# The same operations of a fused retention and FP4 feed-forward kernel in another order on all four engines

## What is computed

```python
q, k = rope(x @ Wq), rope(x @ Wk)
scores = einsum('bhqd,bhkd,hqk->bhqk', q * DQK ** (-0.5), k, decay)   # causal
o = einsum('bhqk,bhkd->bhqd', scores, v)
o = o * rsqrt(mean(o * o) + EPS) * g_norm_w
x = layernorm(x + (o * silu(x @ Wg)) @ Wo)
def fp4_quant_dequant(x):          # blocks of 16
    scale = max(abs(xb)) / 6.0
    return GRID[searchsorted(MID, abs(xb / scale))] * sign(xb) * scale
gate, up = fp4_linear(x, w_gate), fp4_linear(x, w_up)        # 128 -> 352
x = layernorm(x + fp4_linear(silu(gate) * up, w_down))       # 352 -> 128
```

## Time and profile before

| | |
|---|---|
| median of 3 runs | 142.82 us (141.59 to 142.87) |
| profiled execution | 142.74 us, of it the span 140.8 us |
| mean granted TensorE clock, share of full speed | 0.971 |
| PE busy | 125.6 us (89%) |
| DVE busy | 117.9 us (84%) |
| ACT busy | 99.6 us (71%) |
| POOL busy | 101.4 us (72%) |

### The profile page before, as it was taken

One profiled execution on the slowest core, in us unless ns is written; L12 is line 12 of the kernel. 1 busy time (PEld: TensorE's weight loads), 2 busy tenths in 40 slices (PEclk: granted clock), 3 DMA queues, 4 the chain that ended last, 5 costly groups with the idle time before them and its releaser, 6 DMA issues.

```text
span 140.8 us, 3621 instructions
## 1 busy us (share of the span) xinstructions
PE 125.6 (89%) x1232; PEld 81.4 (58%) x1232; DVE 117.9 (84%) x391; ACT 99.6 (71%) x311; POOL 101.4 (72%) x139
## 2 busy tenths in 40 slices
PE   4997898999999989999999899999997789985770
PEld 4864354755565655465566566565767577663650
DVE  1239987598588999999999999999999999999510
ACT  3054966768977778775977778787488689777643
POOL 4204198695997995887989598798967938874741
PEclk9999999999999999999999999999999999999855
DMA  4898970000000000000000000000000000002121
GB/s 122 243 240 244 416 232 3 0 9 0 5 0 0 7 0 0 7 0 0 5 0 2 0 5 0 0 7 0 5 0 0 19 19 2 19 0 79 37 74 56
DMA packets 6897, 6.53 MB, mean 46 GB/s; under 512 B 864, under 2 KB 6112, under 8 KB 6752
## 3 DMA queue, kind: packets, MB, share of 16 engines
q1 hardware_dynamic: 5856, 5.56, 13.3%
q10 hardware_dynamic: 1024, 0.76, 1.7%
HBM read 5.26 MB, written 1.05 MB: 45 GB/s over the span
## 4 chain that ended last, share of the span: by engine, by line
DVE 60%; PE 27%; issue 6%; ACT 2%; POOL 2%; POOLq 0%; DVEq 0%
DVE h_ratio L676 6%; DVE h_ratio L671 6%; PE ps L327 5%; DVE hs L663 5%; DVE h_blocks L821 4%; DVE h_ratio L680 4%; DVE probs L760 3%; PE ps L315 3%; DVE x_ratio L671 3%; PE ps L321 3%; DVE gate_o L780 3%; PE ps L377 2%; DVE x_ratio L676 2%; PE ps L344 2%; DVE ms L775 2%
## 5 line engine op out<-in xcount | busy, mean ns | idle before, releaser
L917 POOL TENSOR_TENSOR rstd_h<-ms,minus_half 128x8 f32<-128x8 f32 x16 | 27.1, 1695 | 9.2 <-DVE ms L775 9.1
L451 PE MATMUL ps<-wd_T,hT 128*128 128x128 f32 x96 | 15.5, 302 | 3.5 <-DVE r L803 2.8
L327 PE MATMUL ps<-w_vg,xT_sb 128*128 128x512 f32 x32 | 17.2, 619 | 0.6 <-DVE h_blocks L821 0.4
L908 POOL TENSOR_TENSOR qk<-rope_c,rope_s 128x256 f32<-128x256 f32 x16 | 12.3, 772 | 7.0 <-DVE rope_s L754 3.5
L944 POOL TENSOR_TENSOR hq<-h_ratio,hs 128x352 f32<-128x352 f32 x16 | 14.2, 898 | 3.6 <-DVE h_ratio L680 3.6
L451 PEld LDWEIGHTS ps<-wd_T,hT 128*128 128x128 f32 x96 | 13.3, 207 | 5.8 <-DVE r L803 3.1
L912 POOL TENSOR_SCALAR_AFFINE_SELECT probs<-raw 128x512 f32<-128x512 f32 x16 | 11.3, 705 | 5.7 <-ACT raw L493 5.7
L928 POOL TENSOR_TENSOR rstd<-veps,minus_half 128x1 f32<-128x1 f32 x16 | 9.6, 597 | 5.3 <-DVE veps L792 5.0
L437 PE MATMUL ps<-wgu_T,xqT 128*128 128x352 f32 x32 | 12.9, 484 | 0.6 <-DVE h_blocks L821 0.3
L431 PE MATMUL ps<-wgu_T,xqT 128*128 128x352 f32 x32 | 12.4, 470 | 0.1
L344 PE MATMUL ps<-q_eo,kT 32*128 32x256 f32 x128 | 11.4, 425 | 1.0 <-DVE gate_o L780 0.5
(11 more groups left out here) (112 smaller groups left out, 357.5 us busy)
## 6 DMA issues: line engine op xcount, KB each, us to landing
tabs_sb<-rope_tables SPq DMA_DIRECT2D x1, 1024.0 KB, 11.4
out<-x SPq DMA_DIRECT2D x16, 64.0 KB, 1.5
tabs_sb<-rope_tables SPq DMA_DIRECT2D x1, 640.0 KB, 7.9
xT_sb<-x_transposed SPq DMA_DIRECT2D x1, 512.0 KB, 9.2
x_res<-x SPq DMA_DIRECT2D x1, 512.0 KB, 11.9
xT_sb<-x_transposed SPq DMA_DIRECT2D x1, 320.0 KB, 6.9
...
```

What stands on the lines that cost most here:

```text
L327: mm(vg_ps, xT(c), w_vg[:], start=True, stop=True).then_inc(vg_pe, 1)
L451: last = mm(down_ps, hT[:, c % D, t, :], wd_T[:, t, :], start=t == 0, stop=t == 2)
L908: gp.tensor_tensor(qk[:, c % D, :], rope_c[:, c % D, :], rope_s[:, c % D, :], ALU.add).then_inc(qk_p, 1)
L917: gp.tensor_tensor(rstd_h[:, c, :], ms[:, c, :], minus_half[:], ALU.pow).then_inc(rms_p, 1)
```

## The change

Every engine's list is a permutation of the old one: no call is added, dropped or given other operands. In VectorE's and GpSimd's lists GpSimd's products and its select stand in other places relative to VectorE's steps with two operands in SBUF. Of the PSUM banks `yT` and `down` are exchanged (0 and 1), the gate weights' transposes move from bank 0 to 3, the up weights' from 3 to 0 and the down weights' from 2 to 3. In the diff "..." marks calls or lines left out.

```diff
-        BANKS = {"scV": (0, 1), "scA": (2, 3), "oT": (4, 5), "o": (2,), "yT": (0,), "qk": (7,),
+        BANKS = {"scV": (0, 1), "scA": (2, 3), "oT": (4, 5), "o": (2,), "yT": (1,), "qk": (7,),
...
-                 "up": (6,), "down": (1,), "U": (4,)}
+                 "up": (6,), "down": (0,), "U": (4,)}
...
-        wg_T_ps, wu_T_ps = ps[:, 0, 0:I], ps[:, 3, 0:I]
-        wd_T_ps = ps[:, 2, 0:384]
+        wg_T_ps, wu_T_ps = ps[:, 3, 0:I], ps[:, 0, 0:I]
+        wd_T_ps = ps[:, 3, 0:384]
...
-                occupy("wgu", (0, 3))
+                occupy("wgu", (3, 0))
...
-                occupy("wdt", (2,))
+                occupy("wdt", (3,))
...
# TensorE: the start and the end
-            project_vg(1); project_qk(1); scores(0); project_vg(2); project_qk(2); from_state(0); values(0)
-            transpose_qk(1); transpose_o(0); state_product(1); project_vg(3); scores(1); from_state(1)
+            project_vg(1); project_qk(1); scores(0); from_state(0); project_qk(2); project_vg(2); values(0)
+            transpose_qk(1); transpose_o(0); state_product(1); project_vg(3); transpose_qk(2); scores(1)
...
-            gate(14); up(14); down(10); transpose_xq(15); transpose_h(11); gate(15); up(15); transpose_h(12); down(11)
-            transpose_h(13); down(12); transpose_h(14); down(13); down(14); transpose_h(15); down(15)
+            down(8); gate(13); up(13); transpose_xq(14); down(9); gate(14); transpose_h(10); up(14); transpose_xq(15)
+            down(10); transpose_h(11); gate(15); up(15); down(11); transpose_h(12); transpose_h(13); down(12)
+            down(13); transpose_h(14); down(14); transpose_h(15); down(15)
...
# ScalarE: the start
-            silu_g_(2); copy_v(2); copy_oT(0); q_even(1); squares(0); weights_magic(1); q_odd(1); k_transposed(1)
+            copy_v(2); silu_g_(2); copy_oT(0); k_transposed(1); q_odd(1); weights_magic(1); squares(0); q_even(1)
...
# VectorE: the start
-            rope_sin_even(0); rope_cos(0); rope_sin_odd(0); next_state(0); weights_amax(0); rope_sin_even(1)
-            rope_sin_odd(1); rope_cos(1); weights_amax(1); mask_scores(0); weights_inv(1); rope_sin_odd(2)
-            rope_cos(2); rope_sin_even(2); weights_inv(0); weights_ratio(1); weights_ratio(0); gated(0)
-            weights_plus(1); next_state(1); weights_grid(1); mean_square(0); weights_value(1); mask_scores(1)
+            rope_cos(0); rope_sin_odd(0); rope_sin_even(0); weights_amax(0); weights_inv(0); next_state(0)
+            rope_cos(1); rope_sin_even(1); rope_sin_odd(1); weights_amax(1); mask_scores(0); rope_sin_odd(2)
+            rope_cos(2); rope_sin_even(2); weights_inv(1); weights_ratio(1); weights_ratio(0); weights_plus(1)
+            gated(0); mean_square(0); next_state(1); weights_grid(1); weights_plus(0); weights_value(1)
...
# VectorE: the end
-            h_product(13); ln2_sum(9); h_plus_(12); h_amax(13); h_grid_(12); h_inv(13); h_product(14); h_ratio_(13)
-            h_amax(14); ln2_sum(10); h_inv(14); h_plus_(13); h_ratio_(14); h_grid_(13); h_product(15); h_plus_(14)
-            ln2_sum(11); h_amax(15); h_grid_(14); h_inv(15); h_ratio_(15); ln2_sum(12); h_plus_(15); h_grid_(15)
+            x_grid_(14); h_amax(12); ln2_sum(8); h_inv(12); x_ratio_(15); h_ratio_(12); h_product(13); x_plus_(15)
+            h_plus_(12); x_grid_(15); h_grid_(12); h_amax(13); ln2_sum(9); h_inv(13); h_product(14); h_ratio_(13)
+            h_amax(14); ln2_sum(10); h_inv(14); h_plus_(13); h_ratio_(14); h_grid_(13); h_product(15); ln2_sum(11)
+            h_amax(15); h_plus_(14); h_inv(15); h_grid_(14); h_ratio_(15); ln2_sum(12); h_plus_(15); h_grid_(15)
...
# GpSimd: the end
-            ln2_rstd(6); ln2_rstd(7); h_value(11); h_value(12); ln2_rstd(8); h_value(13); h_value(14); ln2_rstd(9)
-            ln2_rstd(10); h_value(15); ln2_rstd(11); ln2_rstd(12); ln2_rstd(13); ln2_rstd(14); ln2_rstd(15)
+            h_value(12); ln2_rstd(6); ln2_rstd(7); h_value(13); ln2_rstd(8); ln2_rstd(9); h_value(14); ln2_rstd(10)
+            h_value(15); ln2_rstd(11); ln2_rstd(12); ln2_rstd(13); ln2_rstd(14); ln2_rstd(15)
```

More of the change, by code:

```diff
@@ L866, in _ @@
-            mean_square(13); x_grid_(9); ln1_aggr(11); h_product(6); x_ratio_(10); gated(13); h_amax(6); x_plus_(10)
-            h_inv(6); ln1_sum(12); h_ratio_(6); ln1_stats(12); mean_square(14); ln1_eps(11); gated(14); h_product(7)
-            x_grid_(10); h_amax(7); h_plus_(6); next_state(14); h_inv(7); ln1_aggr(12); ln1_sum(13); h_ratio_(7)
-            mask_scores(15); h_grid_(6); x_amax(11); h_product(8); ln1_eps(12); ln1_stats(13); x_inv(11); h_amax(8)
-            x_ratio_(11); h_inv(8); h_plus_(7); h_ratio_(8); ln1_sum(14); ln2_sum(0); h_grid_(7); ln1_stats(14)
@@ new lines, in _ @@
+            rope_sin_even(9); rope_sin_odd(9); gated(6); ln1_stats(4); h_product(0); mean_square(6); mask_scores(7)
+            h_amax(0); ln1_sum(5); h_inv(0); ln1_aggr(4); h_ratio_(0); mask_scores(8); next_state(6); ln1_stats(5)
+            x_amax(3); ln1_eps(4); h_plus_(0); rope_sin_odd(10); x_grid_(2); rope_cos(10); x_inv(3); x_ratio_(3)
+            x_amax(4); rope_sin_even(10); x_inv(4); ln1_aggr(5); mask_scores(9); ln1_eps(5); ln1_sum(6); h_grid_(0)
+            x_ratio_(4); ln1_stats(6); mean_square(7); h_product(1); next_state(7); h_amax(1); x_plus_(3); gated(7)
@@ new lines, in _ @@
+            h_inv(1); x_plus_(4); ln1_aggr(6); h_ratio_(1); x_grid_(3); rope_sin_odd(11); rope_sin_even(11)
+            ln1_eps(6); x_amax(5); rope_cos(11); x_inv(5); h_plus_(1); x_ratio_(5); mask_scores(10); h_grid_(1)
+            next_state(8); h_product(2); mean_square(8); h_amax(2); gated(8); x_grid_(4); x_plus_(5); ln1_sum(7)
+            x_amax(6); rope_cos(12); rope_sin_even(12); h_inv(2); gated(9); rope_sin_odd(12); x_inv(6); h_ratio_(2)
+            mean_square(9); mask_scores(11); next_state(9); ln1_stats(7); h_plus_(2); x_ratio_(6); x_grid_(5)
@@ new lines, in _ @@
+            h_grid_(2); x_plus_(6); ln1_aggr(7); h_product(3); ln1_eps(7); h_amax(3); mask_scores(12); h_inv(3)
+            ln1_sum(8); h_ratio_(3); next_state(10); rope_cos(13); mean_square(10); x_amax(7); h_plus_(3)
+            rope_sin_even(13); ln1_stats(8); rope_sin_odd(13); ln1_aggr(8); x_grid_(6); ln1_eps(8); x_inv(7)
+            ln1_sum(9); x_ratio_(7); h_grid_(3); ln1_stats(9); gated(10); h_product(4); next_state(11); h_amax(4)
+            ln1_aggr(9); x_amax(8); mean_square(11); h_inv(4); x_plus_(7); h_ratio_(4); x_inv(8); x_grid_(7)
@@ new lines, in _ @@
+            gated(11); rope_sin_even(14); x_ratio_(8); h_plus_(4); rope_cos(14); ln1_sum(10); rope_sin_odd(14)
+            x_plus_(8); ln1_stats(10); mask_scores(13); h_grid_(4); h_product(5); next_state(12); h_amax(5)
+            ln1_eps(9); gated(12); h_inv(5); ln1_sum(11); h_ratio_(5); mean_square(12); ln1_aggr(10); x_grid_(8)
+            x_amax(9); h_plus_(5); x_inv(9); mask_scores(14); ln1_eps(10); x_ratio_(9); h_grid_(5); rope_cos(15)
+            rope_sin_even(15); rope_sin_odd(15); mean_square(13); h_product(6); next_state(13); ln1_stats(11)
@@ new lines, in _ @@
+            gated(13); h_amax(6); x_amax(10); h_inv(6); x_plus_(9); h_ratio_(6); x_inv(10); ln1_aggr(11); ln1_sum(12)
+            x_grid_(9); x_ratio_(10); ln1_stats(12); gated(14); mean_square(14); h_product(7); x_plus_(10); h_amax(7)
+            h_plus_(6); h_inv(7); ln1_eps(11); ln1_sum(13); h_ratio_(7); x_grid_(10); mask_scores(15); h_grid_(6)
+            next_state(14); x_amax(11); ln1_aggr(12); x_inv(11); h_product(8); x_ratio_(11); ln1_eps(12); h_amax(8)
+            ln2_sum(0); h_plus_(7); h_inv(8); ln1_sum(14); h_ratio_(8); mean_square(15); gated(15); h_product(9)
```

222 lines of the change are left out of this document (101 added, 121 removed).

## The result

The changed kernel takes 136.84 us (median of 4 runs, 136.27 to 139.16) against 142.20 us (median of 4, 140.84 to 142.87) for the kernel before. The ratio is 0.9621, with an interval of 0.9508 to 0.9735: 5.4 us faster, where 2.8 were forecast. The profiled execution took 136.37 us, its span is 134.5 us instead of 140.8.

A forecast was written before the change was run, and what follows sets the result against it. VectorE never pauses from 50 to 131 us, TensorE close behind until 100. Terms -0.6-1.2-1.0 = -2.8 us take the profiled 142.74 to 139.9, 140.0 for the median; forecast's own range 138.6 to 141.5, whole range 136.5 to 143.8.

The forecast's parts named there:

- rival (a): Separating VectorE's two-input steps from GpSimd's products works in full: 4 to 5.8 us back, 136.4 to 138.2 us; chance 0.17.
- The sign named for the forecast: Lines 671, 676, 680 of `h_ratio` and `x_ratio` would sum to about 4.5 us above their medians, from 7.2.
- Start: VectorE's `weights_amax(0)` and `weights_inv(0)` ahead of `next_state(0)`, `weights_inv(1)` behind `rope(2)`: scores of chunk 1 earlier, -0.6 us.
- Separation: Over the chunks, fewer VectorE two-input steps under GpSimd products: 1.9 us by positions, -1.2 taken, capped by TensorE's idle time.
- The count by position: Exposure of VectorE's two-input steps after each release of a GpSimd product or select: 9.4 us before, 7.0 after, worth 1.9.
- Rival (b): No net effect: GpSimd's queue sets most starts, so separated pairs meet again; 141.5 to 143 us, chance 0.22.
- The last microseconds: VectorE's last five microseconds: `h_plus(14)` and `h_ratio(15)` escape GpSimd's products, 0.44 and 0.55 us back, -1.0 in sum.
- Drain: The last 9.8 us, draining the last chunks at a mean granted clock of 0.58; no gain was forecast there.
- Banks: New PSUM banks for `yT`, `down` and the transposed weights: cost 0, as all the scores wait for both halves anyway.
- (c): Path from `x_grid` to `h_product` too short in the last five chunks, VectorE waits 2.8 us: 145.0 us, chance 0.16.
- Powers: GpSimd's powers (line 932), unlike its products, were taken not to lengthen VectorE's two-input steps; no size given.

The follow-up runs named there:

- the last experiment: Changed kernel with mean_square(0) ahead of gated(0) on VectorE, so that the power rms_rstd(0) is released earlier: 136.33 us (6 runs), ratio 0.9613.

## Why the prediction was right and where it was wrong

The direction, the range (136.5 to 143.8, of which the 136.84 us are close to the edge) and the mechanism hold: lost time of VectorE's two-operand steps against GpSimd's products, given back by other positions. Taking the competition away moved the two orders to within 0.6 to 1.0 us of each other. The size was off by 2.6 of 5.4 us, on the side of rival (a), whose 136.4 to 138.2 holds the result and whose mechanism is a separation that works in full. The sign named for the forecast, 4.5 us of loss left in the five groups (7.2-1.9-1.0 is 4.3), came out at 2.6, between it and the sign of rival (a), means at their medians. At full clock the change is 4.4 us, so 1.0 of the 2.6 us is clock and 1.6 is the order.

*Start, -0.6.* Right for the edit named: alone it gave 0.5 to 0.9 us at equal clocks, and 0.49 us from scores(0) to scores(1). That scores(1) went from 16.25 to 15.67 us, as forecast, is in part luck: 0.32 of it lie ahead of scores(0), and only 0.25 between the two. One thing on the way was wrong: VectorE's `weights_amax(0)` waited 2.73 us for its transfer until 8.50, where I had the weights landed at about 7, and the first state step slipped from 8.92 to 10.02. scores(0) didn't suffer from it. The stage up to `mask_scores(7)` gave 1.68 us in all. Of these 0.3 lie ahead of the first scores (10.15 to 9.83), whose start differs by more between kernels with the same beginning; some 0.5 are the work moved behind the mark, no gain; and 0.5 agree with the edit's. The 0.43 us of stretch that went there explain nothing, since their removal alone gave 0.03 us in the old order without competition. The last 0.3 to 0.4 us stay open.

*Separation, -1.2.* The middle gave -1.12, so the number was right by luck. I had capped it by TensorE's idle time of 1.2 us; without the competition 2.57 us came through the same stage, while TensorE's idle time fell only from 1.12 to 0.19. So a TensorE that is listed as 98% busy here was not at its floor: 1.6 us of what is listed as busy gave way when its inputs came earlier. In the new order 2.32 us of stretch went and 1.12 us of time. Of the 1.2 between, VectorE's waits took 0.24 (0.03 to 0.27), two small steps more between the marks some 0.3, and `h_product` and `mean_square` got longer by 0.19 and 0.17 in sum; the last 0.3 I can't place.

The count by position gave 1.9 us for all chunks, and I entered 1.2, the part ahead of 100 us; the 0.5 behind it was left out of the sum. The count was low besides: mean less median fell by 4.6 us, where the separation and the last steps together were put at 2.9. It took each product to start 0.15 us after its release. But in the trace of before GpSimd was idle ahead of only 3 of 16 products of `h`, and 3 of 16 of `x`; the others came straight out of its queue, at a time that no position shows. Rival (b) had seen this, and drew from it that separation would come to nothing, which was wrong as well: of the 27 stretched steps 8 were left. The step of the prediction that failed in size is this count. It gave 2.4 us of exposure where 4.9 us of stretch went.

*The last microseconds, -1.0.* The two swaps alone gave 0.8 us at full clock, with both steps at 0.51 us, as walked. The stage from `mask_scores(15)` on, however, gave 2.06, with 2.16 us of stretch gone. What went wrong is that I walked through its last 5 us and left the 29 us ahead of them to the count, though the prediction itself said that VectorE is alone from 100 us on, so that each nanosecond there counts in full. It does: -2.16 gives -2.06 here, with two steps more in the stage, and -2.20 gives -2.20 in the kernel with the new order from 98 us.

*Drain, no term.* 1.42 us of the two profiles' difference lie behind the last `h_grid`, where the clock was 0.58 in the one and 1.00 in the other. All of it is the clock of the profiled run of before, since the old order at full clock has a drain of 4.91 us, shorter than the new one's 5.17. I took the 0.58 as a property of the kernel, and did not ask what the other runs had: 141.59 and 142.82 us lie on two clock levels and are not scatter. The runs of after are at 0.996 to 1.000; why the new order keeps the clock up is not shown. The runs of the last experiment go down to 0.990 and lose nothing by it (136.19 to 136.46 us).

*Banks, 0.* Not shown either way; their one run could not tell.

*The rivals (b) and (c)* would have shown as VectorE below 49 of 50 us, or as new waits of `h_product`. It is at 49.73, and from 100 to 125.5 us at 25.50 of 25.50. The path that (c) feared took 4.86 us in chunk 15 (`x_grid` at 118.28, `h_product` at 123.14) against 5.29 before (121.53 and 126.82), and nothing waited for it:

```profile
123.14 0.51 DVE L823 TENSOR_TENSOR h_blocks<-ps,silu_h 128x352 f32<-128x352 f32 x1
123.36 0.79 POOL L946 TENSOR_TENSOR hq<-h_ratio,hs 128x352 f32<-128x352 f32 x1 [1.32 <-PE ps L443]
...
124.22 0.51 DVE L676 SCALAR_TENSOR_TENSOR h_ratio<-h_magic,h_ratio 128x352 f32<-128x352 bf16 x1
```

These three rows are the old pair of 127.04 and 127.25 taken apart: the product is over before line 676 begins.

*Powers.* "Do nothing of the kind" was right for VectorE, and half of the story. In the traces of before and after 29 and 39 two-operand steps start under a running power (and under nothing else of GpSimd's), and none is over 0.02 us longer than undisturbed; in the other direction the power waits for VectorE. The Trainium skill (SBUF — State Buffer, Who interferes with whom) says that the two exclude each other for the whole of an instruction. For products the runs agree, up to the last 0.13 us of the product. For powers they agree in one direction: VectorE first holds the power up (3.31 instead of 1.65 us), the power first does not stretch VectorE (0.88 and 0.89 us, undisturbed 0.88).
